# Third layer of a four-layer network: score pass for row sums, normalised exponentials, head pairs in 64-row halves, one PSUM ring

## What is computed

```python
def _L2_attn_ref(x, Wq, Wk, Wv):
    ...
    Q = (x @ Wq.T).reshape(b, n, H, R)          # H = 8 heads, R = 64
    K = (x @ Wk.T).reshape(b, n, H, R)
    V = (x @ Wv.T).reshape(b, n, H, d)          # d = 128
    attn = jnp.einsum('bnhr,bmhr->bhnm', Q, K)
    attn = jax.nn.softmax(attn, axis=-1)
    out = jnp.einsum('bhnm,bmhd->bnd', attn, V)  # summed over the heads
    ...
def _L2_ffn_ref(x, w1_w, w1_s, w2_w, w2_s, h1_w, h1_s, h2_w, h2_s, w3_w, w3_s):
    ...
    h = jax.nn.silu(_tlin(x, w1_w, w1_s)) * _tlin(x, w2_w, w2_s)
    h = jax.nn.gelu(_tlin(h, h1_w, h1_s), approximate=False)   # 512 x 512
    h = jax.nn.gelu(_tlin(h, h2_w, h2_s), approximate=False)   # 512 x 512
    return _tlin(h, w3_w, w3_s)
```

## Time and profile before

| | |
|---|---|
| median of 3 runs | 2109.81 us (2108.24 to 2114.43) |
| the profiled execution: its own time, its span | 2104.47 us, 2102.6 us |
| TensorE matmul busy | 1796.5 us, 85% |
| VectorE, ScalarE, GpSimd busy | 1135.1, 925.1, 273.4 us |
| third layer's block | 799 to 1726 us of the span |

### The profile page before, as it was taken

How to read it: one execution, slowest core, us unless ns; L and a number is a source line. 1 busy time by engine, 2 the same in 40 slices (tenths; PEclk the granted TensorE clock), 3 DMA queues, 4 the chain that set the end, 5 groups by cost and what they waited for, 6 DMA issues and landing times. The chain is left out here.

```text
span 2102.6 us, 23302 instructions
## 1 busy us (share of the span) xinstructions
PE 1796.5 (85%) x7982; PEld 1032.2 (49%) x7982; DVE 1135.1 (54%) x1905; ACT 925.1 (44%) x1080; POOL 273.4 (13%) x159
## 2 busy tenths in 40 slices
PE   6699999983289996989899898989898996999996
PEld 3222222222144444666758585766667573444442
DVE  4445445437645556464453727264645535767765
ACT  4567677753022235353534344343535343444342
POOL 0000000002000004020200202020202003322321
PEclk8799999986599998999999999989999998999998
DMA  1222123310043310000000000000000010000000
GB/s 66 43 41 41 41 51 56 56 66 40 22 101 90 87 23 1 1 1 1 1 0 0 0 0 0 0 0 0 0 0 0 0 48 0 0 0 0 0 0 40
DMA packets 18927, 48.30 MB, mean 23 GB/s; under 512 B 640, under 2 KB 1408, under 8 KB 17856
## 3 DMA queue, kind: packets, MB, share of 16 engines
q1 hardware_dynamic: 18496, 47.53, 9.6%
q0 software_dynamic: 384, 0.13, 0.0%
HBM read 45.17 MB, written 2.36 MB: 23 GB/s over the span
## 5 line engine op out<-in xcount | busy, mean ns | idle before, releaser
L493 ACT ACTIVATE probs<-ps_ring 128x1024 f32<-128x1024 f32 x256 | 246.1, 1023 | 126.0 <-PE ps_ring L707 123.3
L1587 PEld LDWEIGHTS ps_o<-v,probs 128*128 128x128 f32 x2048 | 237.4, 192 | 4.9
L1587 PE MATMUL ps_o<-v,probs 128*128 128x129 f32 x2048 | 237.8, 275 | 0.0
L1404 DVE TENSOR_REDUCE max<-ps_o 128x1 f32<-128x512 f32 x256 | 167.9, 687 | 72.6 <-PE ps_o L1482 71.3
L1386 ACT ACTIVATE probs<-ps_wide 128x1024 f32<-128x1024 f32 x128 | 127.8, 1025 | 158.6 <-PE ps_wide L1492 158.5
L721 PE MATMUL ps_o<-probs,v 128*32 128x512 f32 x1024 | 141.5, 627 | 13.1 <-DVE o_sb L544 13.1
L1449 DVE RECIPROCAL rden<-ps_o 128x2 f32<-128x2 f32 x128 | 15.2, 160 | 244.9 <-PE ps_o L1587 244.9
L1350 ACT ACTIVATE probs<-ps_wide,pack 128x512 f32<-128x512 f32 x64 | 40.6, 685 | 212.2 <-PE ps_wide L1544 138.9
L1296 POOL TENSOR_TENSOR ql<-probs,qq 64x2048 fp32r<-64x2048 f32 x16 | 78.8, 4927 | 413.9 <-DVE qq L1422 411.6
L1544 PE MATMUL ps_wide<-probs,pack 128*128 128x512 f32 x256 | 121.6, 592 | 0.0
L1482 PE MATMUL ps_o<-kk,qq 128*128 128x512 f32 x256 | 117.9, 490 | 3.2
(11 more groups left out here) (349 smaller groups left out, 3385.0 us busy)
## 6 DMA issues: line engine op xcount, KB each, us to landing
cwb<-combine_by_expert SPq DMA_DIRECT2D x8, 2048.0 KB
score<-score_by_expert SPq DMA_DIRECT2D x8, 2048.0 KB, 13.7
pack<-pack_dram SPq DMA_DIRECT2D x1, 2560.0 KB, 13.8
pack<-pack_dram SPq DMA_DIRECT2D x1, 2443.0 KB, 9.5
x<-x_in SPq DMA_DIRECT2D x2, 1024.0 KB, 6.0
out<-x SPq DMA_DIRECT2D x1, 2048.0 KB, 6.3
pack<-pack_dram SPq DMA_DIRECT2D x1, 1547.0 KB, 8.1
pack<-pack_dram SPq DMA_DIRECT2D x1, 1288.5 KB, 16.5
```

Source lines behind the costliest of these rows:

```text
L493: nc.scalar.activation(probs[n % 3][:, 2 * half:2 * half + 2, :], ps, ACT.Exp, scale=float(HD0) ** -0.5).then_inc(read, 1)
L1404: nc.vector.reduce_max(top[:, u // NBLK, u % NBLK:u % NBLK + 1], ps_o[1][:, u % 2, :], AX_X).then_inc(max_read, 1)
L1587: last = nc.tensor.matmul(out, probs[:, (h + 1) % 2, m, n * P:(n + 1) * P], v[:, m, h, :], start=(m == 0), stop=(m == NBLK - 1))
```

## The change

In `layer2_mix`:

- q and k keep their layout from the projection: two heads (a pair) in rows 0 to 63 and 64 to 127. ScalarE writes the high part of a whole block (`take_high`), VectorE the low part (`take_low`); nothing is stacked. Score matmuls have 64 rows, and the two heads of a pair follow each other, each into its own bank.
- A first score pass, queries by keys (`denominators`, 6 matmuls for each pair and query block), gives VectorE the negated maximum over both heads' keys (`maximum`, one reduction of 2 x 512) and ScalarE the row sum of exponentials by the sum output of the activation (`sums`). The shift minus maximum minus logarithm of the sum (`make_shift`) is split in high and low, turned on TensorE (`turn_shift`), copied and sent by two DMAs of SyncE's queue into rows 0, 1 and 64, 65 of `sh_row`.
- The second pass, keys by queries (`scores`), is 6 matmuls plus 2 that add the shift through a matrix of ones in those rows; its exponentials are the finished probabilities. `times_v` takes the values stationary and 512 probabilities moving, in float32, and sums all heads and key blocks in one bank (`ps_acc`); VectorE adds it to x.
- The second hidden layer and w3 use split operands and one-pass products; their weights move to `third`, which the previous layer splits. VectorE splits both hidden layers (`split_hidden`). Silu becomes tanh: one more product on VectorE.
- All large PSUM uses go through one ring of three pairs of banks in the order of `ring_order2`. All loops over batches and pairs are written out.
- GpSimd keeps only the low part of x.

```diff
+        "h2_2": tiles_of_rows(f["L2_ffn_h2_w"].T),
+        "w3_2": tiles_of_rows(f["L2_ffn_w3_w"].T),
...
-        "h2_2": tiles_of_rows(f["L2_ffn_h2_w"].T),
-        "w3_2": tiles_of_rows(f["L2_ffn_w3_w"].T),
+        "two_ones2": k["two_ones"],
...
+RING2 = 3
+PAIRS = H2 // 2
+DEN_AT = {0: (0, 1), 1: (2,), 2: (3,)}
+def ring_order2():
+    order = []
+    for b in range(B):
+        for i in range(2):
+            order += [("q", b, i), ("gate", b, 2 * i), ("k", b, i), ("gate", b, 2 * i + 1)]
+        order += [("v", b, 0), ("h1", b, 0), ("h1", b, 1), ("v", b, 1), ("h2", b, 0), ("h2", b, 1)]
+        order += [("den", b, 0, 0), ("den", b, 0, 1), ("v", b, 2), ("den", b, 0, 2), ("v", b, 3), ("den", b, 0, 3)]
+        for p in range(PAIRS):
+            for m in range(NBLK):
+                if p + 1 < PAIRS:
+                    order += [("den", b, p + 1, n) for n in DEN_AT.get(m, ())]
+                order.append(("score", b, p, m))
+    return order
...
+        @block.sync
+        def _(sp):
+            sp.wait_ge(rows_zero, 2)
+            for b in range(B):
+                for p in range(PAIRS):
+                    n = b * PAIRS + p
+                    sp.wait_ge(rows_ready, n + 1)
+                    if n >= 2:
+                        sp.wait_ge(ring_done[turn_of["score", (n - 2) // PAIRS, (n - 2) % PAIRS, NBLK - 1] % RING2],
+                                   turn_of["score", (n - 2) // PAIRS, (n - 2) % PAIRS, NBLK - 1] // RING2 + 1)
+                    for j in range(2):
+                        sp.dma_start(sh_row[n % 2][64 * j:64 * j + 2, :].rearrange("l (m t) -> l m t", t=P),
+                                     rows[8 * j:8 * j + 8, :]).then_inc(sh_loaded[n % 2], 16)
...
+            def tanh(b, t):
+                ps, _ = filled(act, ("gate", b, t))
+                n = b * FT + t
+                if n >= 2:
+                    act.wait_ge(raw_ready, n - 1)
+                nc.scalar.activation(th[:, t % 2, :], ps[:, 0, :], ACT.Tanh, scale=half_s1[:, t:t + 1]).then_inc(tanh_ready, 1)
...
+            def sums(b, p, m):
+                n = b * PAIRS + p
+                act.wait_ge(max_ready, n * NBLK + m + 1)
+                if m == 0 and n:
+                    act.wait_ge(shift_ready, n)
+                ps, read = filled(act, ("den", b, p, m))
+                for j in range(2):
+                    last = nc.scalar.activation(ps[:, j, :], ps[:, j, :], ACT.Exp, bias=negmax[:, j, m:m + 1],
+                                                accum_out=den[:, j, m:m + 1])
+                last.then_inc(read, 1)
+                if m == NBLK - 1:
+                    act.drain()
+                    nc.scalar.activation(lnden[:, :, :], den[:, :, :], ACT.Ln).then_inc(ln_ready, 1)
+            def exponent(b, p, m):
+                n = (b * PAIRS + p) * NBLK + m
+                if n >= 3:
+                    act.wait_ge(pv_done, n - 2)
+                ps, read = filled(act, ("score", b, p, m))
+                slot = 2 * (n % 3)
+                nc.scalar.activation(probs[:, slot:slot + 2, :], ps, ACT.Exp).then_inc(read, 1)
...
+                nc.scalar.preload_act_table_set("natural_log_exp_and_others")
+                sums(b, 0, 0)
+                sums(b, 0, 1)
                 take_v(b, 2)
+                sums(b, 0, 2)
                 take_v(b, 3)
+                sums(b, 0, 3)
+                for p in range(PAIRS):
+                    for m in range(NBLK):
+                        if p + 1 < PAIRS:
+                            for n in DEN_AT.get(m, ()):
+                                sums(b, p + 1, n)
+                        exponent(b, p, m)
...
+            def take_low(b, name, i):
+                n = b * 4 + 2 * i + "qk".index(name)
+                dve.wait_ge(high_ready, n + 1)
+                ps, read = filled(dve, (name, b, i))
+                nc.vector.tensor_tensor(single(low[name][:, 2 * i:2 * i + 2, :]), ps, high[name][:, 2 * i:2 * i + 2, :],
+                                        ALU.subtract).then_inc(read, 1)
+            def take_gate(b, t):
+                dve.wait_ge(tanh_ready, b * FT + t + 1)
+                ps, read = filled(dve, ("gate", b, t))
+                nc.vector.scalar_tensor_tensor(raw[:, t % 2, :], th[:, t % 2, :], 1.0, ps[:, 0, :], ALU.add, ALU.mult
+                                               ).then_inc(raw_ready, 1)
+                dve.drain()
+                nc.vector.scalar_tensor_tensor(raw[:, t % 2, :], ps[:, 1, :], s12[:, t:t + 1], raw[:, t % 2, :], ALU.mult, ALU.mult
+                                               ).then_inc(read, 1)
+                dve.drain()
                 nc.vector.tensor_copy(single(gate_high[:, t, :]), raw[:, t % 2, :])
                 dve.drain()
+                nc.vector.tensor_tensor(single(gate_low[:, t, :]), raw[:, t % 2, :], gate_high[:, t, :], ALU.subtract
+                                        ).then_inc(gate_ready, 1)
+            def split_hidden(b, of, into, done):
+                for i in range(2):
+                    was_read(dve, (of, b, i))
+                    tiles = slice(2 * i, 2 * i + 2)
+                    nc.vector.tensor_copy(single(into[0][:, tiles, :]), hidden[:, tiles, :])
+                    dve.drain()
+                    nc.vector.tensor_tensor(single(into[1][:, tiles, :]), hidden[:, tiles, :], into[0][:, tiles, :],
+                                            ALU.subtract).then_inc(done, 1)
+            def maximum(b, p, m):
+                n = b * PAIRS + p
+                if m == 0 and n:
+                    dve.wait_ge(ln_ready, n)
+                ps, _ = filled(dve, ("den", b, p, m))
+                nc.vector.reduce_max(negmax[:, :, m], ps, AX_X, negate=True).then_inc(max_ready, 1)
+            def make_shift(b, p):
+                n = b * PAIRS + p
+                dve.wait_ge(ln_ready, n + 1)
+                nc.vector.tensor_tensor(shift[:, :, :], negmax[:, :, :], lnden[:, :, :], ALU.subtract)
+                dve.drain()
+                if n:
+                    dve.wait_ge(turned, n)
+                nc.vector.tensor_copy(single(split[:, :, 0, :]), shift[:, :, :])
+                dve.drain()
+                nc.vector.tensor_tensor(single(split[:, :, 1, :]), shift[:, :, :], split[:, :, 0, :], ALU.subtract
+                                        ).then_inc(shift_ready, 1)
+                dve.wait_ge(turned, n + 1)
+                if n:
+                    dve.wait_ge(sh_loaded[(n - 1) % 2], 32 * ((n - 1) // 2 + 1))
+                nc.vector.tensor_copy(single(rows[:, :]), ps_y[0:4 * NBLK, 0:P]).then_inc(rows_ready, 1)
...
+            def denominators(b, p, m):
+                if m == 0:
+                    for name in "qk":
+                        was_read(pe, (name, b, p // 2))
+                ps, done = empty(pe, ("den", b, p, m))
+                block_m = slice(m * P, (m + 1) * P)
+                for n, (lhsT, rhs) in enumerate(((low["q"], high["k"]), (high["q"], low["k"]), (high["q"], high["k"]))):
+                    for j in range(2):
+                        last = nc.tensor.matmul(ps[:, j, :], single(lhsT[head_rows(j), p, block_m]), single(rhs[head_rows(j), p, :]),
+                                                start=(n == 0), stop=(n == 2))
+                last.then_inc(done, 1)
+            def turn_shift(b, p):
+                n = b * PAIRS + p
+                pe.wait_ge(shift_ready, n + 1)
+                if p == 0:
+                    pe.wait_ge(y_added, b + 1)
+                else:
+                    pe.wait_ge(rows_ready, n)
+                nc.tensor.transpose(ps_y[0:4 * NBLK, 0:P], split[:, :, :, :].rearrange("p j l m -> p (j l m)"),
+                                    ident).then_inc(turned, 1)
+            def scores(b, p, m):
+                n = b * PAIRS + p
+                if m == 0:
+                    pe.wait_ge(sh_loaded[n % 2], 32 * (n // 2 + 1))
+                ps, done = empty(pe, ("score", b, p, m))
+                block_m = slice(m * P, (m + 1) * P)
+                for i, (lhsT, rhs) in enumerate(((low["k"], high["q"]), (high["k"], low["q"]), (high["k"], high["q"]))):
+                    for j in range(2):
+                        nc.tensor.matmul(ps[:, j, :], single(lhsT[head_rows(j), p, block_m]), single(rhs[head_rows(j), p, :]),
+                                         start=(i == 0), stop=False)
+                for j in range(2):
+                    last = nc.tensor.matmul(ps[:, j, :], single(two_ones[head_rows(j), :]), single(sh_row[n % 2][head_rows(j), :]),
+                                            start=False, stop=True)
+                last.then_inc(done, 1)
+            def times_v(b, p, m):
+                n = (b * PAIRS + p) * NBLK + m
+                was_read(pe, ("score", b, p, m))
+                if p == 0 and m == 0:
+                    was_read(pe, ("v", b, NBLK - 1))
+                    if b:
+                        pe.wait_ge(acc_added, b)
```

(47 more changed lines are left out.)

427 lines of the change are left out of this document (134 added, 293 removed).

## The result

| | before | changed |
|---|---|---|
| median | 2110.05 us (4 runs, 2108.24 to 2114.43) | 2217.19 us (4 runs, 2209.1 to 2219.78) |
| profiled execution: own time, span | 2104.47, 2102.6 us | 2209.1, 2207.3 us |
| TensorE busy | 1796.5 us | 1852.3 us |
| VectorE, ScalarE, GpSimd busy | 1135.1, 925.1, 273.4 us | 1038.8, 1003.1, 153.4 us |

The changed kernel is slower: ratio 1.0508, 95% interval 1.0487 to 1.0528. The forecast was 2208.0 us with a range of 2110 to 2285.

A forecast was written before the change was run, and what follows sets the result against it. VectorE and ScalarE's chain bounds a batch's first quarter, TensorE's array passes the rest. Profiled 2104.5 + 84 (eight batches, 124.8 against 114.3 us) + 14 (clock) + 5 (weight split) = 2208 us, range 2110 to 2285.

The forecast's parts named there:

- First part: Third-layer batch, first q matmul to first hidden matmul: 21.2 us, against 28.4 before with values 1 in it.
- First hidden layer with the wait behind it: In each batch: matmuls 11.1 us, then 3.7 us for gelu, split and hand-overs before the second hidden layer.
- To the first turn: From the second hidden layer's end to a batch's first turn of the shift: 14.3 us, TensorE standing 4.3 at the end.
- Middle pairs: Head pairs from turn to turn of the shift: 16.6 us each, with 1.5 open transfer wait and 1.2 for form changes.
- First pair: First head pair of a batch, with three values blocks: 15.5 us.
- Last pair: Last head pair of a batch, with no next pair to cover the transfer: 14.7 us.
- rival 4: Clock falls at each of a batch's four waits: 3 x 1.2 us more, +29, 2237 us; in range, no own chance.
- Clock: Half-rate matmuls after TensorE's waits before the first hidden layer and first turn: 1.8 us per batch, 14 us in all.
- Weight split: Beside the batches, splitting two further weights lengthens ScalarE's and GpSimd's work: 5 us, between 3 and 8.
- Halves side by side: Score passes: two 64-row matmuls run together, 0.231 us for a pair, so 224 cost 25.9 us per batch.
- rivals 2 and 3: Score passes: half rows give nothing, 2370 us (chance 0.06); halves only partly side by side, 2270 us (chance 0.10).
- Rival 1: Third-layer batches: shift chains hide and TensorE becomes the bound, 2037 us, 2090 a fair time; chance 0.13.

## Why the prediction was right

The sign, the place and the size hold, and each step can be laid beside its window. The sum was made for the profiled execution: 2208 beside 2209.1 us. That they agree to 1 us is luck, since terms below are off by more in both directions; the median of the four runs is 2217.

- *First part* 21.2 us, measured 20.84, with casts at 0.43. The run with the old splits on VectorE confirms the reading of rows 4.
- *First hidden layer with the wait behind it* 11.1 + 3.7 = 14.8, measured 16.20: behind the 3.48 us wait before it TensorE ran at half rate for some 3.5 us. *Second hidden layer* 11.1, measured 11.11 in this batch; in four of the eight it had a half-rate stretch too.
- *To the first turn* 14.3, measured 13.74, with a wait of 3.78 (4.3 expected).
- *Middle pairs* 16.6, measured 16.57 and 16.61. Errors cancel in them: a change of form costs 0.20 us, not 0.15, so 1.6 us a pair, not 1.2; and the scores start 3.0 us after the turn, not 3.2, so that the open wait for the transfer is 1.15 us, not 1.5. The prediction had 0.20 as its end.
- *First pair* 15.5, measured 15.53, which is luck. The prediction's own terms give 14.6 (16.6 less a values block of 1.72 and two changes of 0.15), and a part of the 15.53 is half rate: with the idle products in one pass the clock holds there and the pair takes 15.24 (1246.69 to 1261.93).
- *Last pair* 14.7, measured 16.25. The walk has no clock in it; behind the 2.74 us wait in this pair the clock is half, and one values block alone takes 2.80 us. This is a part of rival 4, which lay inside the range.
- *Clock*: 1.8 us a batch was taken, and 124.8 + 1.8 = 126.6 compares with 126.85 for the batch shown but with 128.1 for the mean. This term was the mis-sized one. The idle products won 2.9 us a batch at two of the three places, without the last pair, so the true price is nearer rival 4 (1.8 + 3.6) than the term was. The step that failed is "the one before the first hidden layer (3.6) is shorter": that it lies under 4.1 did not save the clock, in any batch, and waits of 2.0 and 2.7 us, which the term leaves out, were followed by half rate in many.
- *Weight split* 5 us between bounds of 3 and 8, measured 3.4, as far as it can be told. The third layer begins at 800.60 instead of 799.73, but this is no measure: it begins anywhere from 800.5 to 809.6 us in the twelve runs in which all layers before it are the changed kernel's, since the first layer's time varies. From a common point behind the first layer, VectorE's copy of `n_prob` (487.06 us after, 490.15 before), to TensorE's last `n_count` product (563.60 and 563.34 us) it is 76.54 us after and 73.19 before, and 76.5 to 76.6 in the other eleven, 73.2 in the run with the old splits on VectorE. Beside it the third layer's first wait, for GpSimd's `xl`, is 6.49 us instead of 5.80. In the profiled execution the 3.1 us by which the first layer happened to be shorter hid the term. GpSimd was busy until 8 us later than before, counted from that copy, and VectorE lost less than half of it (DVE and POOL, time lines of after; compare):

```profile
495.95 2.28 DVE L925 TENSOR_TENSOR n_tie<-n_first,n_prob 128x2048 f32<-128x2048 f32 x1
498.31 2.29 DVE L928 TENSOR_REDUCE n_mass<-n_tie 128x256 f32<-128x2048 f32 x1
500.67 13.93 DVE L931 TENSOR_SCALAR n_mass<-n_mass 128x256 f32<-128x256 f32 x1
497.55 16.89 POOL L912 TENSOR_TENSOR w_low<-pack,w_high 128x7680 fp32r<-128x7680 f32 x1 [127.91 <-ACTq L828]
```

  GpSimd waits for ScalarE's longer high part, so it begins 2.1 us later, counted from the copy. The first of the two 2.3 us operations was under way by then, and the second, a reduction, ran beside GpSimd at its usual 2.29 us. Before, the first came 0.5 us behind GpSimd's start and was held. In both kernels VectorE is held once, until GpSimd ends.
- *Halves side by side* at 0.231: shown by the run with both on one half. The rate of the Trainium skill's page that the prediction cites (3.07 of 4, for four tiles) does not show here at two tiles of 64 rows. Its +60 us did not come, and rivals 2 and 3 fall.
- *Rival 1*, TensorE as the bound: it would decide when waits and changes of form are gone. The runs that removed one at a time (66 for the transfer, 27 at the first turn, 24 for the clock, 30 for the form) do not reach the kernel before (2110) alone, and the best order of the same work gave 2135. All of them together were not tried. Only with the values in one pass, which is less work and less precise, did the new attention pass the kernel before.

So the change is several changes. Taking GpSimd from VectorE's way is worth 54 us and can be had alone; the rest, the new attention above all, compared with that, costs 161 us (2217 - 2056).

## What to carry to other kernels

Before a rewrite is given credit, take its cheapest part alone: moving three splits to another engine made the kernel 54 us faster, where the whole change made it 107 us slower. Where a result must leave an engine and come back (a row that is turned, copied and sent), count what the waiting engine has between the request and its use, and move finished work there; it was worth 45 us without touching the transfer. When the values products were grouped to save changes of form, the buffers that had been enough for single blocks became the bound, so a saving in slots is to be checked against the ring's depth.

## What was not expected of the hardware

- Six 64-row matmuls for two row halves take three slots of 0.23 us also when the three of one half come first in the code: the other half's first product then starts within 0.01 us of the first half's, and before its second.
- Ten idle matmuls (2.4 us) in a wait of 3.5 us make the kernel faster: 23.5 us for two such places a batch.
- The length of one wait does not tell what the clock does behind it. Half rate followed waits of 3.5 to 4.1 us in all sixteen places of the changed kernel, but in the run with the turn before the values two of eight waits of 3.5 us had full clock for the next 3.6 us. Waits of 2.75 us were followed by half rate in seven of eight batches, of 2.0 us in four of eight; and in the run with the turn before the values, waits of 2.5 to 2.9 us in one of eight (granted clock 0.59 from 989.06).
- VectorE's reduction over 128 x 2048 took 2.29 us beside GpSimd's subtraction, as alone, where an operation of 256 columns that takes 0.29 us alone was held for 13.93 us.
- The output of a sum adds an own record of 0.19 us to an exponential, but only 0.09 us to the distance to the next (0.68 us where the record of the sum starts at 0.59).
